# First pass over the edges of a graph layer: the 32-column query addition moves from VectorE to GpSimd

## What is computed

```python
k = jnp.concatenate([Kn, ek], axis=1).reshape(-1, H, DK)      # H = 4 heads, DK = 56
q = jnp.concatenate([Qn, eq], axis=1).reshape(-1, H, DK)
att = jnp.einsum('ehd,ed->eh', k, q.sum(axis=1)) / SQRT_DK
v = jnp.concatenate([Vn, ek], axis=1).reshape(-1, H, DK)
...
att, v = edge_msgs(K[row], Q[col], V[row], e1, e2)
att_i, v_i = edge_msgs(K[col], Q[row], V[col], e2, e1)
att = seg_softmax(att, col, n)
att_i = seg_softmax(att_i, row, n)
```

## Time and profile before

| | |
|---|---|
| median of 3 runs | 6172.16 us (6169.42 to 6180.93) |
| the profiled execution, its own time | 6190.15 us |
| its span, first to last instruction | 6188.2 us |
| first pass, in the span | about 2157 to 4893 us |
| POOL busy in the whole span | 3356.0 us (54%) |
| DVE busy in the whole span | 3605.8 us (58%) |

### The profile page before, as it was taken

The page is one execution under the profiler, slowest core; times in us unless marked ns, Lnnn a source line. Parts: engine busy times, 40 slices in busy tenths (PEclk is TensorE's granted clock), DMA queues, the critical chain, the costliest instruction groups (busy, mean ns, idle before and its releaser), DMA issues. The chain is left out here.

```text
span 6188.2 us, 65823 instructions
## 1 busy us (share of the span) xinstructions
PE 3600.1 (58%) x19041; PEld 2528.6 (41%) x19154; DVE 3605.8 (58%) x7770; ACT 2052.3 (33%) x4450; POOL 3356.0 (54%) x3131
## 2 busy tenths in 40 slices
PE   6634555455438755554555555454555399955784
PEld 5522323233225333333333333333433288844674
DVE  8763444344422466666676667676767477766414
ACT  6522222222211144444444444444544222202222
POOL 0176665665530067667676676676667465524242
PEclk5555655555568566666666666666666599977797
DMA  5144655565300166655566555555556599838464
GB/s 137 57 131 133 174 169 159 161 172 158 117 6 3 33 178 194 173 160 172 167 179 185 162 164 162 160 165 164 162 161 164 133 311 314 307 93 280 134 198 161
DMA packets 585556, 992.63 MB, mean 160 GB/s; under 512 B 140634, under 2 KB 380574, under 8 KB 585187
## 3 DMA queue, kind: packets, MB, share of 16 engines
q0 software_dynamic: 151824, 411.87, 22.3%
q1 hardware_dynamic: 336106, 328.02, 19.7%
q10 hardware_dynamic: 97273, 248.52, 11.9%
HBM read 612.43 MB, written 375.69 MB: 160 GB/s over the span
## 5 line engine op out<-in xcount | busy, mean ns | idle before, releaser
L1450 POOL DMA_INDIRECT kv_a<-kvq_rows,rec_a x904 | 966.2, 1069 | 722.1 <-DMA rec_a<-records 393.6
L626 POOL DMA_INDIRECT records<-stage,pos x806 | 882.6, 1095 | 774.7 <-DVE stage L872 540.9
L1458 POOL DMA_INDIRECT messages<-stg_a,rec_a x904 | 923.7, 1022 | 516.9 <-issue 267.0
L1608 PE MATMUL psA_a<-pay_a,oh_a 128*128 128x260 f32 (+1 forms) x1808 | 818.8, 630 | 0.6 <-ACT wout_a L1479 0.6
L1601 PE MATMUL small_a<-ident,top_a 5*128 5x5 f32 x226 | 57.4, 254 | 1273.6 <-DVE top_a L1579 875.6
L1608 PEld LDWEIGHTS psA_a<-pay_a,oh_a 128*128 128x128 f32 x1808 | 539.4, 312 | 131.4 <-issue 1.3
L1601 PEld LDWEIGHTS small_a<-ident,top_a 5*128 5x128 f32 x226 | 37.6, 166 | 1316.9 <-DVE top_a L1579 897.6
L858 DVE TENSOR_TENSOR pick<-psO,oh 128x357 f32<-128x357 f32 x248 | 113.0, 498 | 738.6 <-remote 436.6
L671 ACT ACTIVATE rings<-psE 128x512 bf16<-128x512 f32 x496 | 233.2, 516 | 903.8 <-remote 700.2
L1578 DVE TENSOR_TENSOR_SCAN fwd_a<-flag_a,small_a 4x128 f32<-4x128 f32 x226 | 91.2, 404 | 752.1 <-remote 725.8
L1824 PE MATMUL psA_b<-msg_b,oh_b 128*128 128x260 f32 x1808 | 451.6, 394 | 1.6 <-DVE msg_b L1779 1.4
(11 more groups left out here) (493 smaller groups left out, 9012.4 us busy)
## 6 DMA issues: line engine op xcount, KB each, us to landing
messages<-zimg ACTq DMA_DIRECT2D x56, 2080.0 KB
msg_b<-messages ACTq DMA_DIRECT2D x56, 2080.0 KB
win_a<-kvq_rows SPq DMA_DIRECT2D x226, 236.0 KB
WA<-in_L_ffn_w_dram SPq DMA_DIRECT2D x66, 512.0 KB
part_rows<-wout_a SPq DMA_DIRECT2D x226, 132.5 KB
rings<-lo_keys SPq DMA_DIRECT2D x124, 208.0 KB
kv_a<-kvq_rows,rec_a POOLq DMA_INDIRECT x904
messages<-stg_a,rec_a POOLq DMA_INDIRECT x904
```

Source lines behind the costliest of these rows:

```text
L626: pool.indirect_dma_start(out=rec_d, out_offset=bass.IndirectOffsetOnAxis(ap=pos1[:, t:t + 1], axis=0), in_=stage[:, t, :], in_offset=None ...
L1450: pool.indirect_dma_start(out=kv[u][:, j, :], out_offset=None, in_=kvq_d, in_offset=bass.IndirectOffsetOnAxis(ap=at[:, j, 4:5], axis=0)).t ...
L1458: pool.indirect_dma_start(out=msg_d, out_offset=bass.IndirectOffsetOnAxis(ap=at[:, j, 5:6], axis=0), in_=stg[t % 4][:, j, :], in_offset=No ...
L1608: mm = nc.tensor.matmul(psA[:, 0:n], oh[t % 2][:, :], pay[t % 2][:, j, 0:n], start=j == 0, stop=j == W - 1)
```

## The change

After the four fetches of tile s+2 and before the four scatters of tile s-1, POOL waits in step s for the third sine of tile s (`s_e1`) and adds the 32 sine columns of the fetched rows to the last 32 query columns of the same rows (128 partitions x 4 edges x 32 columns, f32, in place), and raises a new semaphore `s_kq`. DVE drops its addition (L1571) and waits for `s_kq` at its place.

```diff
+        s_kq = sem("s_kq")
...
                         pool.indirect_dma_start(out=kv[u][:, j, :], out_offset=None, in_=kvq_d,
                                                 in_offset=bass.IndirectOffsetOnAxis(ap=at[:, j, 4:5], axis=0)).then_inc(s_kv[u], 16)
+                t = s
+                if ok(t):
+                    k = kv[t % KVS]
+                    q = k[:, :, KVQ - TD:KVQ]
+                    pool.wait_ge(s_e1, t + 1)
+                    nc.gpsimd.tensor_tensor(q, q, k[:, :, PROJ:PROJ + TD], ALU.add).then_inc(s_kq, 1)
                 t = s - 1
                 if ok(t):
                     pool.wait_ge(s_att2, t + 1)
...
                     q = k[:, :, KVQ - DK:KVQ]
-                    link(nc.vector.tensor_tensor(q[:, :, DK - TD:DK], q[:, :, DK - TD:DK], k[:, :, PROJ:PROJ + TD], ALU.add))
+                    dve.wait_ge(s_kq, t + 1)
                     kc = ctrA[u][:, 0:PROJ - DK + TD].rearrange("p (h d) -> p h d", d=DK)
```

## The result

The changed kernel takes 6237.61 us (median of four, 6213.53 to 6259.07) where the kernel before takes 6170.79 us (four runs, 6136.4 to 6180.93): a ratio of 1.0117, 95% interval 1.0063 to 1.0171, or +67 us. The forecast was 6305 us, +133 us. Two later comparisons gave 1.0103 (1.0057 to 1.0149; 6209.35 against 6144.05 us) and 1.0149 (1.0126 to 1.0171; 6291.34 against 6191.20 us): +65 and +100 us. All three intervals lie above 1, so the sign is certain; the size lies between half and three quarters of the forecast.

The account below looks back on a forecast made before the run. The prediction took POOL's own line in the first pass to bound the kernel. Addition and gap, 0.59 us x 226 tiles = +133 us, with POOL's waits unchanged, gave 6305 us against the median 6172; range 6090 to 6470 us.

Parts of the forecast that it names:

- POOL's line sets the pace: First pass: POOL has 10.95 us of its own a tile, which the addition lengthens to 11.54; chance 0.46.
- The addition's 0.44 us and its gap of 0.15: POOL's queue between fetches and scatters: addition plus gap in front, together 0.59 us a tile, bounds 0.22 and 1.37.
- The two waits behind a long wait, set against each other: POOL after a long wait: sine 1.5 us later than DVE's sum, against 1.54 us payload wait saved; counted as nothing.
- DVE's dropped addition: DVE's L1571 removed: some 0.3 us a tile of DVE's time, nothing on the end, as DVE idles 3.25 us a tile.
- its new wait: DVE's second half waits for POOL's addition, some 2 to 3 us a tile before L1573; by itself costs nothing.
- The faster one: Rival: DVE can't run ahead, so POOL's long waits go; 6048 us, or 6113 if three quarters go; chance 0.26.
- The coupling rival: POOL meets a long wait every 4 tiles instead of 4.7, each costing 7.4 us; +294 us, 6466 us; chance 0.12.
- The exclusion: Rival: POOL's addition waits out DVE's long product L1550 in every tile; +382 us, 6554 us; chance 0.04.
- No change, something behind POOL: Rival: DMA traffic or PE's delay sets the pace, so 0.59 us fills POOL's waiting; 6172 us; chance 0.12.

Follow-up runs that it names:

- the kernel with the addition first: The changed kernel with POOL's wait and addition of tile s ahead of the fetches of tile s+2: 6213.37 us, 1.0094 to the kernel before.
- the waits alone: The changed kernel, but POOL writes one number instead of adding and DVE adds behind its wait: 1.0040 and 1.0024 to the kernel before.
- the fill: The kernel before plus a zero fill of 128 x 128 numbers on POOL's queue, awaited by nobody: 6205.40 against 6191.20 us, 1.0021.
- more cover for POOL: The kernel before with each scatter a step later (tile s-2) and six message buffers instead of four: 6320.48 us, 1.0277.
- POOL's own addition: The kernel before plus a same-size addition on POOL's queue, on buffers of its own, DVE keeping its addition: 1.0278 and 1.0289.

## Why the prediction was right, and where its terms were off

**POOL's line sets the pace.** Shown on chips without long waits: POOL waits for nobody and its busy and issue time fill the pass; an addition that nobody needs costs +149 and +155 us, the coupling without the addition +14 and +10 us. On chips with them, where the change itself was measured, it rests on the accounts below and on the kernel with the addition first. There the split of POOL's 2500 us into tiles, from the groups of each profile, is this (us a tile; before is the mean of two profiles, after of three):

| | DMAs busy | addition | issue | waits for others | tile |
|---|---|---|---|---|---|
| before (6190 and 6196 us) | 8.24 | 0 | 2.60 | 1.29 | 12.1 |
| after (6241, 6179 and 6310 us) | 8.16 | 0.60 | 2.36 | 1.25 | 12.4 |

**The addition's 0.44 us and its gap of 0.15.** The sum, 0.59 us, meets the measured 0.60 by luck, for both parts are wrong. Where nothing of DVE's is in its way it takes 447 to 466 ns, nearly the estimate; the mean of 600 comes of meeting DVE's products. The Trainium skill (GPSIMD Engine Reference, Elementwise — side-by-side cycle accounting) has about 2.6 cycles an element at 1.2 GHz, an estimate of 0.28 us for 128; the traces show 0.45 at the least, 0.17 us more. Whether that is a fixed part of every instruction no run here shows. The gap in front of the addition is zero where it waits for nobody, and the one behind it is 0.17 instead of 0.30 us: 0.13 us gained a tile where I had put 0.15 lost. This was the first mis-sized term.

**The two waits behind a long wait, set against each other.** Mis-sized, and this is the second term. I had the sine 1.5 us later than the sum, and 1.54 us of payload wait given back. The payload wait did go (issue before a fetch is 0.306 us in the mean, 247.5 / 809, against 0.351 before, 290.8 / 828). The 1.5 us came only by half: at POOL's waits of over 1 us the sine ends 1.5 us after DVE's sum in the kernel before (the median, in both profiles), but 0.7, 0.7 and 0.8 us in the three of the changed kernel (0.73 in the timeline above: 3499.35 against 3498.62). A long wait costs POOL 5.2, 5.0 and 6.0 us (240.6 / 46, 211.8 / 42, 291.8 / 49), against 5.1 and 4.7 (223.8 / 44, 275.6 / 59). The two terms would give back 0.13 + 4 x 0.045 = 0.31 us of issue; the table loses 0.24, since there is 0.04 us of issue in front of the addition, and since a scatter that waited for DVE's sum had no gap of its own to lose. 0.60 - 0.24 leaves 0.36 us a tile, or +81 us, inside the measured +65 to +100 us; the table's DMAs and waits would take another 0.12 us off, but the two profiles of before alone differ by 0.26 us in the one and 0.29 in the other.

**DVE's dropped addition is worth nothing, and its new wait costs nothing.** Right as far as shown: the waits alone cost next to nothing on the chips without long waits, and with more lead for DVE no loss was seen to come back on one with them. I had put 2 to 3 us a tile on the new wait; it is 0.97 on the chip with long waits and 404.6 / 208 = 1.95 with the waits alone on the other kind. That DVE loses its lead in the long waits would explain it, but isn't shown.

**Rivals.** The faster one falls on the chips with long waits: DVE can no longer run ahead, yet 61 waits remain before the scan, and POOL's waits stay at 1.25 us. The coupling rival falls by the waits alone on the other chips. On these its size falls by the long waits' number and price: one in 4.4, 4.9 and 4.1 tiles, 5.0 to 6.0 us each, where it wanted one in 4 and 7.4 us. A smaller part of it isn't ruled out: on the chip of the +100 us POOL waits 1.47 us a tile with the changed kernel and 1.13 with the fill. That is one profile of each, and two of the kernel before differ by nearly as much. The exclusion is real and small: 600 - 450 = 0.15 us a tile on POOL. The Trainium skill (SBUF — State Buffer, SBUF: two separate sides) says that of a GpSimd operation that reads SBUF and a DVE operation with two SBUF inputs the first to start holds the shared ports, and the other waits for its end. The trace agrees that they hinder each other, but not in that form: at 3482.77 DVE's product started first and was itself stretched to 1.35 us, and the addition ended 0.30 us after it, less than it takes alone.

**No change, something behind POOL.** Not the pace: additions aren't absorbed (+1.51 us a tile for 1.74 us of them). But the thing behind POOL exists. On chips with long waits DVE gets PE's results, in the three kernels' timelines shown, 2.3 to 4.1 us after POOL has stopped issuing, and more cover for POOL lengthened the wait instead of hiding it. Over the first pass of the changed kernel 46 of DVE's 55 waits of over 5 us before the scan end 2.0 to 3.1 us after POOL's last instruction, and none later. The rest end sooner, two of them while POOL issues; with the fill 21 of 68 do. So POOL's stop isn't the only thing that ends them.

**What stays open.** What holds PE's results back, and why two of the chips (or the times at which they were used) show none of it: there the view of waits has no wait before the scan at all, in six profiles, and the whole kernel is 15% shorter, other stages included. The changed kernel itself never fell on a chip without long waits, and POOL's addition alone never on one with them; that the first would cost about 2.5 to 3% is an inference from its parts.

## What to carry to other kernels

Before moving work off an engine, split the time of the engine that receives it into busy, issue gaps and waits, per tile: a queue that only issues DMAs and shows a 0.30 us gap before each is full although it looks 70% busy. An addition that VectorE does in 0.28 us inside idle time took 0.60 us on the queue that set the pace, and cost 0.29 to 0.44 us a tile. And a wait that shrinks with more cover in theory should be tried: here the buffers that were to hide it made the kernel 2.8% slower, and in the timeline the wait ended only after the covered engine had stopped.

## What was not expected of the hardware

**The same kernel, 5226 and 6171 us.** The difference isn't in the kernel's text. The profiles, of different kernels, show where it lies: first pass 12.1 us a tile in the kernel before against 10.6 with waits alone, and the stretch of the earlier stage from 400 to 800 us, in which POOL scatters the records, moves 258 GB/s with the waits-alone kernel on a chip without long waits and 152 GB/s with the kernel before on one with them. The two kinds differ by far more than the change, so only ratios on one chip tell of it.

**An indirect DMA that meets DVE's product takes up to twice as long.** In the kernel with POOL's own addition:

```profile
3004.92 0.97 POOL L1466 DMA_INDIRECT messages<-stg_a,rec_a  x1 [0.30 <-issue]
3006.15 1.09 DVE L1560 TENSOR_TENSOR prod_a<-kv_a,q1s_a 128x896 f32<-128x896 f32 x1 [2.00 <-ACT kv_a L1510]
3006.20 1.88 POOL L1466 DMA_INDIRECT messages<-stg_a,rec_a  x1 [0.30 <-issue]
...
3017.42 1.09 DVE L1560 TENSOR_TENSOR prod_a<-kv_a,q1s_a 128x896 f32<-128x896 f32 x1 [2.27 <-ACT kv_a L1510]
3017.73 1.61 POOL L1466 DMA_INDIRECT messages<-stg_a,rec_a  x1 [0.30 <-issue]
```

Started 0.05 us into the product the DMA takes 1.88 us, started 0.31 us into it 1.61 us, and 0.97 us clear of it: it ends 0.8 us after the product (3008.08 and 3019.34 against 3007.24 and 3018.51) both times. So do nearly all of the 207 DMAs that start inside this product (L1560) in this profile: 0.83 us after its end in the median, nine in ten between 0.82 and 0.89. In the waits-alone kernel one that starts 0.65 us into the product takes 1.29 us. POOL's line thus depends on where in the step DVE's product falls. That may be why the kernel that only dropped DVE's addition was 0.6% slower. Its scatters take 1047 ns in the mean, against 980 in the waits-alone kernel, but its fetches 1004 against 1058, together 0.05 us a tile more; and no profile of the kernel before was taken on such a chip, so this isn't shown.
